# Sums of members on TensorE, dense routing weights, and the second bias made in the attention of a one-core transformer block with experts

## What is computed

```
h = tok(x)                             # three levels of patches, Hilbert order, a linear map: 2048 tokens x 192
h = h + attn(layernorm(h))             # linear attention, 12 heads of 16, phi = elu + 1
t = rmsnorm(layernorm(h)) * scale
g = t @ gate_w.T + gate_b              # 16 experts
top_vals, top_idx = top_k(g, 4)
route_w = softmax(top_vals)            # four weights a token
comb    = sum_k onehot(top_idx) * route_w          # dense: 16 columns, 12 of them zero
hid = t @ mlp1_w[e].T + mlp1_b[e]
a   = min(glu, 7) * sigmoid(1.702 * min(glu, 7)) * (clip(lin, -7, 7) + 1)
y   = a @ mlp2_w[e].T + mlp2_b[e]      # mlp2_b: the second bias
out = h + layernorm(h) + sum_e comb[e] * y[e]
```

## Time and profile before

| | |
|---|---|
| median of 3 runs | 506.99 us (506.65 to 512.21) |
| the profiled execution | 506.39 us, span 504.6 us |
| granted TensorE clock | 0.936 of full, mean of the span |
| busy: PE / DVE / ACT / POOL | 404.8 / 309.6 / 261.2 / 251.3 us |
| 250 to 480 us (tile loop) | PE without a gap, clock 1.00 from 250 on |
| 134 to 241 us | 64 scatters on POOL |
| DMA | 49.66 MB, mean 98 GB/s |

### The profile page before, as it was taken

One profiled execution on the slowest core, in us unless ns is written; L12 is line 12 of the kernel. 1 busy time (PEld: TensorE's weight loads), 2 busy tenths in 40 slices (PEclk: granted clock), 3 DMA queues, 4 the chain that ended last, 5 costly groups with the idle time before them and its releaser, 6 DMA issues.

```text
span 504.6 us, 10757 instructions
## 1 busy us (share of the span) xinstructions
PE 404.8 (80%) x2983; PEld 281.0 (56%) x2983; DVE 309.6 (61%) x829; ACT 261.2 (52%) x617; POOL 251.3 (50%) x218
## 2 busy tenths in 40 slices
PE   0455469799999978481699999999999999999920
PEld 0341126666665645230377777777777777777710
DVE  0576776577888887220266776677666666676610
ACT  0639873556667553000356665666566656665510
POOL 7887830000365666656045455555555565555540
PEclk9999996999999997777699999999999999999985
DMA  8999952700122222271234444444444444444335
GB/s 230 252 248 246 270 150 59 213 2 18 33 85 68 85 84 85 83 196 68 79 42 67 69 81 68 69 75 74 68 68 76 73 69 68 68 73 76 42 42 116
DMA packets 43283, 49.66 MB, mean 98 GB/s; under 512 B 7835, under 2 KB 34717, under 8 KB 43229
## 3 DMA queue, kind: packets, MB, share of 16 engines
q1 hardware_dynamic: 25006, 29.93, 23.5%
q0 software_dynamic: 16256, 17.38, 20.3%
q10 hardware_dynamic: 1966, 1.66, 1.2%
HBM read 29.41 MB, written 21.35 MB: 101 GB/s over the span
## 4 chain that ended last, share of the span: by engine, by line
PE 51%; DMA 20%; SPq 11%; DVE 7%; issue 4%; POOL 3%; ACT 1%; POOLq 0%; ACTq 0%; DVEq 0%
DMA xs<-R 16%; PE pair L1258 12%; PE pair L1247 5%; PE pair L1236 5%; PE pair L1240 5%; PE pair L1237 5%; PE pair L1239 5%; PE pair L1238 5%; SPq L266 3%; PE pair L1219 3%; SPq L267 2%; DMA W2s<-in_m 2%; SPq L265 2%; POOL xs L354 2%; PE pair L1261 1%
## 5 line engine op out<-in xcount | busy, mean ns | idle before, releaser
L705 DVE TENSOR_SCALAR R<-pair 128x384 f32<-128x384 f32 x79 | 44.1, 558 | 91.6 <-PE pair L1240 91.6
L368 POOL DMA_INDIRECT out<-R x40 | 64.4, 1610 | 65.7 <-ACT R L946 65.7
L368 POOL DMA_INDIRECT acc_odd<-R x39 | 62.7, 1608 | 52.7 <-ACT R L946 52.7
L354 POOL DMA_INDIRECT xs<-R x64 | 62.7, 980 | 37.2 <-DMA xs<-R 28.8
L1258 PE MATMUL pair<-W2s,R 128*128 x711 | 71.6, 246 | 0.8 <-ACT R L946 0.8
L934 ACT ACTIVATE R<-pair 128x384 f32<-128x384 f32 x79 | 38.8, 491 | 60.2 <-PE pair L1240 60.2
L1258 PEld LDWEIGHTS pair<-W2s,R 128*128 128x128 f16 x711 | 60.6, 98 | 2.1 <-issue 1.0
L928 ACT ACTIVATE R<-pair 128x384 f16<-128x384 f16 x79 | 38.1, 483 | 40.1 <-PE pair L1219 40.1
L315 POOL DMA_INDIRECT R<-in_x,idx_sb x42 | 51.4, 1224 | 13.6 <-issue 12.5
L1240 PE MATMUL pair<-W1s,R 67*128 x158 | 52.2, 330 | 0.0
L1236 PE MATMUL pair<-W1s,R 128*128 x158 | 52.1, 330 | 0.0
(11 more groups left out here) (237 smaller groups left out, 764.2 us busy)
## 6 DMA issues: line engine op xcount, KB each, us to landing
R<-xs SPq DMA_DIRECT2D x79, 104.5 KB, 2.0
W1s<-in_m1a SPq DMA_DIRECT2D x14, 384.0 KB
W2s<-in_m SPq DMA_DIRECT2D x14, 288.0 KB
W1s<-in_m1c SPq DMA_DIRECT2D x14, 192.0 KB
acc_odd<-lz SPq DMA_DIRECT2D x17, 96.0 KB, 1.8
W1s<-W1s SPq DMA_DIRECT2D x1, 1536.0 KB, 10.1
out<-h_all SPq DMA_DIRECT2D x8, 192.0 KB, 2.2
out<-acc_odd POOLq DMA_DIRECT2D x1, 1536.0 KB, 10.7
```

Of the source, the lines that this page charges most:

```text
L354: po.indirect_dma_start(out=xs, out_offset=bass.IndirectOffsetOnAxis(ap=sl_i[:, q, n:n + 1], axis=0), in_=rowb[:, q, j, :], in_offset=None ...
L368: po.indirect_dma_start(out=(out, acc_odd)[t % 2], out_offset=bass.IndirectOffsetOnAxis(ap=li, axis=0), in_=yv[:, t % 4, :], in_offset=Non ...
L705: ve.tensor_scalar(lin[:, p, :], bank[2 + 2 * p][:, 0:HID], (LIMIT + 1) * S1, (1 - LIMIT) * S1, ALU.min, ALU.max).then_inc(s_lin, 1)
```

## The change

Members are no longer summed on POOL. `ranks` and `counts` add the members of all earlier tiles in TensorE's accumulation, with one matmul for each batch's tile. POOL keeps only the scatters; the row-number copy goes to VectorE. The weights are made dense: the exponential of all 16 gates less the top one, times the members, over their sum. The second bias leaves the tile loop: TensorE transposes the 16 weights of each row (`comb_transposes`), ACT copies them, TensorE multiplies with `B2` (`second_bias`), ACT copies the result, and SP stores it to `acc_odd`, in place of the zeros. In the tile loop three waits and the range checks of the expert number go, and the last matmul. Fillers are fewer, and the 40 ahead of the loop become 28 behind the 58th scatter.

```diff
-ROWC = D1 + 5
+ROWC = D1 + 3
@@ sync
-            for t in range(NT + 1):
-                sp.dma_start(acc_odd[t * P:(t + 1) * P, :], lz[:, :]).then_inc(s_zd, 16)
+            sp.dma_start(acc_odd[ROWS:ROWS + P, :], lz[:, :]).then_inc(s_zd, 16)
...
+            def store_bias(b):
+                sp.wait_ge(s_ys, b + 1)
+                sp.dma_start(av_odd[:, 2 * b:2 * b + 2, :], ys).then_inc(s_yd[b % 2], 16)
+
             for b in range(NB):
                 sp.wait_ge(s_base, b + 1)
                 sp.dma_start(ov[:, 2 * b:2 * b + 2, :], h_all[:, 2 * b:2 * b + 2, :]).then_inc(s_based, 16)
+                if b >= 2:
+                    store_bias(b - 2)
             store_pads(sp, range(0, NE // 2))
+            store_bias(NB - 2)
+            store_bias(NB - 1)
@@ gpsimd
-                if b < NB - 1:
-                    po.wait_ge(s_mr, b + 1)
-                    po.tensor_tensor(Mall[:, b + 1, :], Mall[:, b, :], Mx[:, 2 * b, :], ALU.add).then_inc(s_ma, 1)
...
-                po.tensor_copy(rowb[:, q, :, D + NE:D + NE + 1].bitcast(I32),
-                               idx_sb[:, 42 + 2 * b:42 + 2 * b + 2].rearrange("p (t n) -> p t n", n=1)).then_inc(s_idr, 1)
-                po.wait_ge(s_idr, b + 1)
@@ vector, low_rows and weights
+                ve.tensor_copy(rowb[:, b % BUFS, :, D + NE:D + NE + 1].bitcast(I32),
+                               idx_sb[:, 42 + 2 * b:42 + 2 * b + 2].rearrange("p (t n) -> p t n", n=1))
...
-                link(ve, ve.tensor_reduce(es[:, :], ew[:, p, :, :], AX.X, ALU.add))
+                link(ve, ve.tensor_tensor(cw[:, :, :], ew[:, p, :, :], Mx[:, 2 * b:2 * b + 2, :], ALU.mult))
+                link(ve, ve.tensor_reduce(es[:, :], cw[:, :, :], AX.X, ALU.add))
                 link(ve, ve.reciprocal(es[:, :], es[:, :]))
...
+                ve.scalar_tensor_tensor(out=rowb[:, b % BUFS, :, D:D + NE], in0=cw[:, :, :], scalar=1.0 / (SA * S2),
@@ scalar, start of step s
+                if s >= 3:
+                    copy_combT(s - 3)
+                if s >= 4:
+                    copy_bias(s - 4)
@@ tensor
+            def comb_transposes(b):
+                pe.wait_ge(s_cb, b + 1)
+                pe.wait_ge(s_gc, b + 1)
+                wait(pe, s_cc, b)
+                for j in range(2):
+                    ins = pe.transpose(bank[7][0:NE, P * j:P * (j + 1)], rowb[:, b % BUFS, j, D:D + NE], ident)
+                ins.then_inc(s_cT, 1)
+
+            def second_bias(b):
+                pe.wait_ge(s_cc, b + 1)
+                wait(pe, s_ys, b)
+                for j in range(2):
+                    ins = mm(bank[0][:, D * j:D * (j + 1)], combT[:, P * j:P * (j + 1)], B2[:, :], start=True, stop=True)
+                ins.then_inc(s_b2, 1)
 ...
             def ranks(b):
                 pe.wait_ge(s_mr, b + 1)
-                pe.wait_ge(s_ma, 2 * b + 1)
...
+                for t in range(2 * b):
+                    mm(o, ones16, Mx[:, t:t + 1, :].broadcast_to([P, 2, NE]), start=False, stop=False)
@@ tensor, end of step s
+                if s >= 2:
+                    comb_transposes(s - 2)
                 if s + 1 < NB:
-                    keep_busy(bank[0], 8 if s == 0 else 5)
+                    wait(pe, s_ys, s - 3)
+                    keep_busy(bank[0], 8 if s == 0 else 5 if s < 3 else 3)
+                if s >= 3:
+                    second_bias(s - 3)
@@ tensor, ahead of the loop
-            keep_busy(bank[1], 40)
+            n = 8 * NB - 7
+            pe.wait_ge(s_sct[n % WAYS], 16 * (n // WAYS + 1))
+            keep_busy(bank[1], 28)
@@ tensor, one tile
-                wait(pe, s_tc, t - 1)
...
-                return bass.ds(pe.value_load(tab[0:1, 0, t:t + 1], min_val=0, max_val=NE - 1), 1)
+                return bass.ds(pe.value_load(tab[0:1, 0, t:t + 1]), 1)
...
-                wait(pe, s_u, t - 1)
...
-                pe.wait_ge(s_alo, t + 1)
                 wait(pe, s_y, t)
+                if t == STEPS - 1:
+                    pe.wait_ge(s_alo, t + 1)
...
-                mm(bank[5][:, 0:D], bcol16, W1s[0:ROWC, e, 3, 0:D], start=False, stop=True).then_inc(s_l2, 1)
+                ins.then_inc(s_l2, 1)
```

More of the change, by code:

```diff
@@ L35 @@
 BUFS = 4
+WAYS = 2
 S1 = 2.0 ** 9
@@ L352, in _ @@
                         n = TOPK * j + k
-                        wait(po, s_sct[n % 2], 16 * (4 * b + n // 2))
+                        i = 8 * b + n
+                        wait(po, s_sct[i % WAYS], 16 * scattered(i, i % WAYS))
                         po.indirect_dma_start(out=xs, out_offset=bass.IndirectOffsetOnAxis(ap=sl_i[:, q, n:n + 1], axis=0),
-                                              in_=rowb[:, q, j, :], in_offset=None).then_inc(s_sct[n % 2], 16)
+                                              in_=rowb[:, q, j, :], in_offset=None).then_inc(s_sct[i % WAYS], 16)
             po.wait_ge(s_tab, 1)
+            for k in range(WAYS):
+                po.wait_ge(s_sct[k], 16 * scattered(8 * NB, k))
+            po.memset(Cb[D1:67, :, :], 1.0).then_inc(s_ms, 1)
+            po.wait_ge(s_zd, 16 * 2)
             for k in range(2):
-                po.wait_ge(s_sct[k], 16 * 4 * NB)
-            po.memset(Cb[D1:67, :, :], 1.0).then_inc(s_ms, 1)
-            po.wait_ge(s_zd, 16 * (NT + 2))
+                po.wait_ge(s_yd[k], 16 * NB // 2)
             po.wait_ge(s_based, 16 * NB)
@@ L610, in weights @@
                 ve.wait_ge(s_ex, b + 1)
-                link(ve, ve.tensor_reduce(es[:, :], ew[:, p, :, :], AX.X, ALU.add))
+                link(ve, ve.tensor_tensor(cw[:, :, :], ew[:, p, :, :], Mx[:, 2 * b:2 * b + 2, :], ALU.mult))
+                link(ve, ve.tensor_reduce(es[:, :], cw[:, :, :], AX.X, ALU.add))
                 link(ve, ve.reciprocal(es[:, :], es[:, :]))
[L613 to L619, removed]
+                ve.scalar_tensor_tensor(out=rowb[:, b % BUFS, :, D:D + NE], in0=cw[:, :, :], scalar=1.0 / (SA * S2),
+                                        in1=es[:, :].rearrange("p (t k) -> p t k", k=1).broadcast_to([P, 2, NE]),
+                                        op0=ALU.mult, op1=ALU.mult).then_inc(s_cb, 1)
                 ve.wait_ge(s_cb, b + 1)
@@ L861, in high_rows @@
                 ac.wait_ge(s_tp, b + 1)
-                for k in range(2):
-                    wait(ac, s_sct[k], 16 * 4 * (b - BUFS + 1))
+                for k in range(WAYS):
+                    if b >= BUFS:
+                        ac.wait_ge(s_sct[k], 16 * scattered(8 * (b - BUFS + 1), k))
                 ac.activation(rows[:, b % BUFS, :, 0:D], tp, ACT.Copy).then_inc(s_th, 1)
@@ L877, in base, with copy_combT, copy_bias @@
                 ins.then_inc(s_base, 1)
+            def copy_combT(b):
+                ac.wait_ge(s_cT, b + 1)
+                wait(ac, s_b2, b)
+                ac.activation(combT, bank[7][0:NE, 0:2 * P], ACT.Copy, scale=SA * S2).then_inc(s_cc, 1)
+            def copy_bias(b):
+                ac.wait_ge(s_b2, b + 1)
+                if b:
+                    ac.wait_ge(s_yd[(b - 1) % 2], 16 * ((b - 1) // 2 + 1))
+                ac.activation(ys, bank[0][:, 0:2 * D].rearrange("p (t n) -> p t n", t=2), ACT.Copy).then_inc(s_ys, 1)
             def exp_top(b):
@@ L921, in _ @@
             store_pads(ac, range(NE // 2, NE))
+            copy_bias(NB - 2)
+            copy_combT(NB - 1)
+            copy_bias(NB - 1)
             ac.wait_ge(s_ms, 4)
@@ L1037, in hn_transposes @@
                 wait(pe, s_hnte, b)
+                wait(pe, s_ys, b - 4)
                 for j in range(2):
@@ L1152, in counts @@
                 pe.wait_ge(s_mr, NB)
-                pe.wait_ge(s_ma, 2 * NB - 1)
                 pe.wait_ge(s_qe, NB)
                 o = bank[3][:, 0:NE]
-                mm(o, ones16, Mall[:, NB - 1, :], start=True, stop=False)
-                mm(o, ones16, Mx[:, NT - 2, :], start=False, stop=False)
-                mm(o, ones16, Mx[:, NT - 1, :], start=False, stop=True).then_inc(s_cn, 1)
+                for t in range(NT):
+                    ins = mm(o, ones16, Mx[:, t, :], start=t == 0, stop=t == NT - 1)
+                ins.then_inc(s_cn, 1)
             for b in range(6):
@@ L1201, in _ @@
             ranks(NB - 1)
+            second_bias(NB - 2)
+            comb_transposes(NB - 1)
+            second_bias(NB - 1)
             keep_busy(bank[1], 8)
@@ L1313 @@
     one[1, D1 + 1] = 1
-    one[1, D1 + 4] = 1
     tail = ns[P:D]
```

58 lines of the change are left out of this document (30 added, 28 removed).

## The result

The changed kernel takes **597.64 us** (median of 4, 595.4 to 599.33) against 506.82 before; the ratio is **1.174, interval 1.168 to 1.179**. I had forecast 497.0 with a range of 490.5 to 502.5, and given slower by over 2% a chance of 0.02. Executions of one kernel fall into a fast and a slow state and ratios here compare fast ones; in the sets of `e5` to `e8` and of `e13` to `e16` slow ones were many (the kernel before had a median of 513 there instead of 507 to 510), and the profiles of `e10` and `e13` are of slow ones, so there I go by periods and stage lengths.

What follows compares the result with a forecast made beforehand. Bound: TensorE's stream in the tile loop and queued scatters before it. Terms 6.5 + 0.5 + 6.0 + 0.7 + 0.35 - 4.4 = 9.65 off 506.39 gave 496.7, stated as 497.0 us; 490.5 to 502.5 holds eight in ten.

Steps and rivals of the forecast that it cites:

- the one on the checks: Tile loop: removed waits and register checks give back only what the period has above its matmuls, 0.5 us, bounds 0 and 1.5.
- the one on the loop: Rival: the tile loop keeps its period because something beside TensorE's stream sets it, 504 us; chance 0.03.
- TensorE's own stream is the bound: Tile loop: TensorE's matmuls follow without a gap and set the period of 2.971 us a tile.
- the matmul that I priced at 6.5 us: Tile loop: one 192-column output matmul fewer a tile, 0.082 us each over 79 tiles, all on the path.
- the estimate by the Trainium skill: Tile loop: 26 matmuls take 2.945 us by that page, leaving 0.026 a tile for waits and checks, 2.1 us in all.
- the gaps of POOL: Scatter stage: two sums and a copy go from POOL at the seven batch boundaries, saving 6.0 us, bounds 4.5 and 6.5.
- the stores: Scatter stage: eight second-bias stores of 192 KB amid the scatters cost 4.4 us, bounds 0 and 15.2.
- Ahead of the first scatter: POOL's copy and the start behind it cost 0.90 us before the first scatter, of which 0.7 goes.
- late batches: Rival: attention steps longer than about 13 us make POOL wait for slots, losing the boundaries' 6.0 us, 500.5 us; chance 0.12.
- the counts and the last slots: After the attention: TensorE's 6.53 us stall goes, counts, pads and last slots come some 6 us earlier; nothing on the path.
- The moved filler: Between scatters and tile loop: 40 fillers become 28 behind scatter 57; counted as nothing, bounds -2.1 and +1.
- the rival of the bridge: Rival: 28 fillers hold the clock to the first tile, saving 2.1 us on first hidden layers, 494.9 us; chance 0.15.

Runs made afterwards that it cites:

- e5: Changed kernel, expert number's range still undeclared, with the three waits of a tile put back: 632.77 us, ratio 1.231, period 4.507 us.
- e8: Changed kernel with range declared unchecked, eight second-bias stores left out, sixteen zero stores put back early: scatter stage 110.1 us.
- e13: Kernel before with only the tenth output matmul of a tile left out (output lacks the second bias): 514.82 us, ratio 0.994, period 2.970 us.
- e16: Changed kernel with range declared and unchecked, run once more beside other variants: 504.18 us, ratio 0.983, scatter stage 110.8 us.
- e10: Changed kernel with the range declared only for the nine output matmuls of a tile: 537.59 us, ratio 1.052, period 3.381 us.
- e1: Changed kernel with the expert number's range 0 to 15 declared again, with its run-time check: 499.46 us, ratio 0.981, period 2.872 us.
- e9: Changed kernel with range and run-time check, and the three waits put back: 505.25 us, ratio 0.989, period 2.973 us.
- e14: Kernel before with only the range's run-time check left out, range still declared: 512.34 us, ratio 0.995, period 2.959 us.
- e6: Changed kernel with range declared unchecked and the three waits of a tile put back: 519.21 us (503.36 to 538.07), period 2.872 us.
- e11: Changed kernel, range declared unchecked, without the eight second-bias stores, sixteen zero stores early; repeat run: scatter stage 101.7 us.
- e3: Changed kernel with the expert number's range declared but not checked at run time: 498.5 us, ratio 0.983, period 2.872 us.
- e7: Changed kernel with range declared unchecked and four semaphores for the scatters instead of two: 528.67 us, ratio 1.032, scatter stage 122.9 us.
- e15: Changed kernel with range declared unchecked and three semaphores for the scatters instead of two: 532.89 us, ratio 1.042, scatter stage 113.5 us.

## Why the prediction was wrong

*The step that failed* is the one on the checks: "with the register checks they can give back only what the period has above its matmuls". I took the edit for a removal of checks and bounded it by a gain of 0 to 1.5 us. It was the opposite: without the declared range there are 19 range checks a tile instead of one, and TensorE's sequencer, which has to issue them, becomes the bound. That cost 98 to 101 us (`e1` against the changed kernel; 1.284 x 79). No rival held it either: the one on the loop only let the period stay. The term had no upper end on the side of a loss, though the edit sat on the queue of the bound engine.

*The reading that failed with it*: "TensorE has no gap ... TensorE's own stream is the bound." The matmuls' rows do touch. But `e9` and `e13` show that the sequencer, with the check and the three waits, sets the 2.973 us, 0.02 above the array. So the terms of the loop do not add up one by one: the matmul that I priced at 6.5 us gives nothing alone (`e13`), the check alone 1.1 (`e14`: 0.014 x 79), and the matmul with either the check or the waits gives 0.101 a tile, 8.0 us (`e6` and `e1`, both at 2.872), where the sum had 7.0. Of the 0.101, 0.082 is the array's and 0.019 what the period stood above the array; the rows had said 0.01 for that, and the estimate by the Trainium skill (TensorE: Matmul & The Clock Gate, Wait — 56ns, not 53.3ns?) 0.026. Both came near in size, and neither tells that the check or the waits must go before any of the 0.082 shows.

*Right in mechanism, off in size*: the gaps of POOL (3.5 for 6.0) and the stores (1.9 for 4.4). Their difference is 1.6 in both, by luck; the stage itself shortened by 2.8 (106.4 to 103.6 on average), and the rest is not accounted for. Ahead of the first scatter I had 0.7: from the end of the list of slots to the scatter it took 1.05 us before and 0.85 after, so 0.2.

*Right, but barely*: late batches did not come. Behind the first batch POOL waits for DMAs and not for slots in the changed kernel, but where the list of slots was 3.1 to 13.8 us early before, it is now 0.9 to 3.7 early in six of seven batches, and 0.4 in batch 6 of `e11`. So this stage has little room left unless the attention gets faster too.

*Wrong, and off the path*: the counts and the last slots did not come 6 us earlier. TensorE's stall ahead of the counts is gone, but they start 78.6 us behind the first scatter, 78.1 before. The same sixteen matmuls of filler stand ahead of the ranks of batch 6 in both kernels, and in the changed one they and the work around them fell into a stretch at the lower clock (0.50 of full from 192.8 to 209.9; before, it was 1.00 from 194.6 to 208.2). The kernel before, then the changed one:

```profile
196.17 3.63 PE L966 MATMUL pair<-W2s,C 128*128 128x512 f16 x16
```

```profile
205.25 5.89 PE L995 MATMUL pair<-W2s,C 128*128 128x512 f16 x16
```

*The moved filler.* From the last landing of the scatters to the first tile's gating (first L705 or L711) it takes 7.8 us before and 7.4 in the changed kernel. There the clock rose at 237.2 under the fillers, but TensorE then stood still from 242.9 to 245.3, and the clock was low again from 247.4 to 250.8. In `e11` it stood still only from 243.1 to 244.0, and in `e16` from 249.9 to 250.2: there the clock stayed up, and the first gating came after 6.0 us. That is the rival of the bridge, with 1.8 us where I had 2.1. In `e6` the fillers began late and ended 6.2 us after the last landing; there the first gating took 9.1. So the same filler helps, does nothing or hurts by when it starts. The changed kernel, then `e11` (busy of PE, PEld, DVE, ACT, POOL; clock; DMA):

```profile
248.00:250.00 2.00, 2.00 (x10) 1.14 (x9) 0.15 (x1) 0.93 (x2) 0.00 (x0) 0.50 0.34 87
```

```profile
248.00:250.00 2.00, 1.71 (x15) 1.04 (x13) 1.79 (x4) 1.20 (x5) 0.00 (x0) 1.00 0.37 102
```

With the range kept, the forecast of 9.65 us less would have looked right: `e1` is 9.5 below the kernel before of its own set (508.99 to 499.46). That is luck. The loop gives 8.0 and the stage 2.8, more than I had, and in the profiles the first scatter starts 6.0 us later in `e1` than before, where I had put it 1 us earlier. My last step of the forecast was also loose: 496.7 and 0.6 are 497.3, not 497.0.

## What to carry to other kernels

An engine that shows no gap may still be bound by its own queue: look at the idle time put down to "issue" on the weight loads behind a register read, and count instructions (page header) as well as busy time. Where a queue is that full, range checks and satisfied waits are priced like work, and taking out one instruction of the array gives nothing until some of them go too. A declared range of a register value can spare checks instead of costing them: here it left one a tile, or none where it was declared unchecked, and without it each indexed matmul had its own. Compare the header's count of instructions before trusting an edit that "removes" something, and ask of what kind the new ones are.

## What the runs showed of the hardware that was not expected

- On TensorE, once its queue is the bound, a range check of a register costs 0.083 us and a satisfied wait 0.117 us; below that point both cost nothing (`e6`, `e3` and `e1` have the same 2.872).
- Each wait put back was an instruction of its own: 231 more for three in 79 tiles (`e5`, `e6`).
- TensorE ran float32 matmuls of 192 columns without a gap from 81.3 us in the changed kernel, and its clock rose to 2.4 GHz only at 93.8; in the kernel before the same stretch began at 81.8 and the clock rose at 85.2. With it the first scatter moved by up to 7 us between kernels with nearly the same instructions there.
- With three or four scatters of 128 rows in flight instead of two, the semaphores of some of TensorE's matmuls rose as much as 7 us after the matmuls' recorded starts, and a batch took 16 us instead of 12 (`e7`; in `e15` the first two).
